# Value products of two tiles side by side, with four probability buffers; maxima over keys by pairs of PSUM banks, with two score banks left

## The reference

```python
B, Lq, H = x_q.shape            # 16, 256, 128
nh = 16; dh = H // nh           # 16 heads of 8
scores = jnp.einsum('bqhd,bkhd->bhqk', q, k) / jnp.sqrt(jnp.float32(dh))
attn = jax.nn.softmax(scores, axis=-1)
out = jnp.einsum('bhqk,bkhd->bqhd', attn, v).reshape(B, Lq, H)
```

## Time and profile before

| what | value |
|---|---|
| median of 3 runs | 6772.17 us (6766.07 to 6781.2) |
| the profiled execution's own time | 6777.38 us |
| its span, first to last instruction | 6775.6 us |
| mean granted TensorE clock | 0.963 of full speed |
| PE busy | 6148.7 us (91%) |
| DVE busy | 4444.0 us (66%) |
| ACT busy | 4234.5 us (62%) |
| POOL busy | 982.1 us (14%) |

### The profile page before, as it was taken

The page is one execution under the profiler, slowest core; times in us unless marked ns, Lnnn a source line. Parts: engine busy times, 40 slices in busy tenths (PEclk is TensorE's granted clock), DMA queues, the critical chain, the costliest instruction groups (busy, mean ns, idle before and its releaser), DMA issues.

```text
span 6775.6 us, 156710 instructions
## 1 busy us (share of the span) xinstructions
PE 6148.7 (91%) x49714; PEld 3142.0 (46%) x49714; DVE 4444.0 (66%) x9848; ACT 4234.5 (62%) x8158; POOL 982.1 (14%) x1660
## 2 busy tenths in 40 slices
PE   6999999999777999999998777799999999979998
PEld 3444444444444444444443344344444444435554
DVE  5777777776555777777775355577777777724333
ACT  3777777777665777777775465566766767642223
POOL 3112112211111111111110011221211211100000
PEclk9999999999998999999999899899999999989998
DMA  2222222221112222222220111222212222101110
GB/s 84 74 71 60 62 76 66 55 73 43 56 56 73 77 66 65 67 73 76 66 64 20 37 56 61 67 56 75 66 52 77 56 63 67 46 32 41 42 42 24
DMA packets 181002, 403.68 MB, mean 60 GB/s; under 512 B 16992, under 2 KB 124560, under 8 KB 166416
## 3 DMA queue, kind: packets, MB, share of 16 engines
q1 hardware_dynamic: 180752, 400.01, 22.0%
HBM read 316.81 MB, written 83.14 MB: 59 GB/s over the span
## 4 chain that ended last, share of the span: by engine, by line
PE 76%; DVE 8%; ACT 6%; issue 6%; DMA 3%; SPq 1%; POOL 1%; DVEq 0%; ACTq 0%; POOLq 0%
PE bank L1112 19%; PE bank L1084 17%; PE bank L1067 16%; DVE MX L1409 3%; DMA QP<-scr_q 3%; PE bank L653 2%; PE bank L1038 2%; PE bank L1033 2%; PE bank L644 2%; PE bank L1099 2%; PE bank L670 1%; PE bank L1088 1%; ACT P L1242 1%; PE bank L582 1%; PE bank L1048 1%
## 5 line engine op out<-in xcount | busy, mean ns | idle before, releaser
L1242 ACT ACTIVATE P<-bank 128x512 f32<-128x512 f32 (+1 forms) x5504 | 3078.5, 596 | 1483.5 <-PE bank L1067 1457.9
L1409 DVE TENSOR_REDUCE MX<-bank 128x1 f32<-128x400 f32 (+1 forms) x6144 | 3214.4, 569 | 1129.9 <-PE bank L1084 1046.9
L1067 PE MATMUL bank<-QP,KP 128*128 128x256 bf16 (+1 forms) x11008 | 2091.0, 277 | 104.2 <-ACT QP L1253 42.9
L1084 PE MATMUL bank<-KP,QP 96*128 96x400 bf16 (+1 forms) x6144 | 2099.1, 342 | 67.6 <-DMA QP<-scr_q 46.7
L1112 PE MATMUL bank<-P,VA 128*25 128x256 f32 (+1 forms) x22016 | 1776.8, 395 | 20.2 <-issue 9.6
L1067 PEld LDWEIGHTS bank<-QP,KP 128*128 128x128 bf16 (+1 forms) x11008 | 1030.2, 101 | 791.0 <-issue 180.0
L1084 PEld LDWEIGHTS bank<-KP,QP 96*128 96x128 bf16 x6144 | 594.2, 97 | 1015.6 <-DVE MX L1409 598.5
L1112 PEld LDWEIGHTS bank<-P,VA 128*25 128x25 f32 (+1 forms) x22016 | 403.8, 102 | 741.7 <-issue 623.8
L1412 DVE TENSOR_REDUCE MX<-bank 128x2 f32<-128x512 f32 x512 | 327.0, 685 | 304.5 <-PE bank L1088 304.4
L1532 POOL COPY VA<-VN 128x416 f32<-128x416 f32 (+1 forms) x320 | 138.9, 434 | 2569.5 <-PE bank L1112 1290.5
L1253 ACT CAST QP<-bank 2x512 bf16<-2x512 f32 x640 | 338.8, 575 | 133.6 <-PE bank L1099 127.6
(11 more groups left out here) (209 smaller groups left out, 4705.5 us busy)
## 6 DMA issues: line engine op xcount, KB each, us to landing
KP<-scr_k SPq DMA_DIRECT2D x192, 900.6 KB
QP<-scr_q SPq DMA_DIRECT2D x960, 48.0 KB
CN<-ctx_n SPq DMA_DIRECT2D x40, 768.0 KB
scr_k<-KSF SPq DMA_DIRECT2D x48, 600.8 KB, 3.3
scr_k<-KSF SPq DMA_DIRECT2D x48, 600.0 KB, 3.4
CT<-ctx_t SPq DMA_DIRECT2D x24, 800.5 KB, 4.4
KP<-scr_ks SPq DMA_DIRECT2D x128, 144.0 KB
scr_q<-QS SPq DMA_DIRECT2D x80, 192.0 KB, 2.1
```

Of the source, the lines that this page charges most:

```text
L1067: last = nc.tensor.matmul(SC[ph.score_bank(2 * (g * ph.nt + t) + half)][0:kt, k * N:(k + 1) * N], KP[g][:, c0:c0 + kt], QP[g][:, h * N:(h ...
L1084: last = nc.tensor.matmul(dst[:, 0:n], QP[g][0:MR, h * N + qt * 128:h * N + qt * 128 + 128], KP[g][0:MR, h * ph.nk + c0:h * ph.nk + c0 + n ...
L1242: nc.scalar.activation(P[v % 2][0:kt, half * 2 * N:(half + 1) * 2 * N], SC[ph.score_bank(2 * (g * ph.nt + t) + half)][0:kt, :], ACT.Exp, s ...
L1409: nc.vector.tensor_reduce(MX[:, r, c:c + 1], src[:, 0:CHUNKS[c][1]], AX.X, ALU.max).then_inc(sem("max_done"), 1)
```

## The change

Three things are changed at once.

- **Value products.** There are four probability buffers (`NP = 4`) in place of two. PE keeps back the value products of a tile and writes those of two tiles one behind the other, in every second tile (where `g * nt + t` is even).
- **Maxima.** Two tensors `MP` of two neighbouring banks each take the place of the three banks `MB`. `maximum` now writes two matmuls of 401 columns, one in each bank of a pair (`SPANS`: the ranges overlap by one key, so that all have 401), and DVE reduces both with one instruction of 2x401 elements. A cross group has 16 of these pairs in place of 32 maxima, a self group 2 (of four matmuls) in place of 4. Pair j waits for the reduction of pair j-2.
- **Scores.** Two score banks are left, one for each half: a score waits for the `Exp` of the same half of the tile before.

`maximum_at` is not edited, but with 16 in place of 32 it now gives the tiles 0 to 10 of a group 2, 1, 2, 1, 2, 1, 2, 1, 2, 1 and 1 pairs, and the third third of a tile, behind the value products, is always empty.

```diff
+NP = 4
+SPANS = [(0, 401), (400, 401), (800, 401), (1200, 401)]
-        self.nm = 2 * G * len(CHUNKS) if self.cross else G
+        self.nm = G * len(SPANS) if self.cross else G // 2
...
-        P = [sb("P%d" % k, [128, G * N], f32) for k in range(2)]
+        P = [sb("P%d" % k, [128, G * N], f32) for k in range(NP)]
...
-        SC, MB, OB, MISC = bank[0:3], bank[3:6], bank[6], bank[7]
+        SC = [ctx.enter_context(nc.psum_tensor("bank%d" % k, [128, 512], f32)) for k in range(2)]
+        MP = [ctx.enter_context(nc.psum_tensor("pair%d" % k, [128, 1024], f32)) for k in range(2)]
...
             def scores(ph, b, g, t, half):
-                u = 2 * (g * ph.nt + t) + half
-                pe.wait_ge(sem("probs_full"), at("probs_full", b, ph.score_before(u) + 1))
+                pe.wait_ge(sem("probs_full"), at("probs_full", b, 2 * (g * ph.nt + t) + half - 1))
...
             def maximum(ph, b, g, j):
-                if j >= len(MB):
-                    pe.wait_ge(sem("max_done"), at("max_done", b, g * ph.nm + j - len(MB) + 1))
-                dst = MB[j % len(MB)]
+                if j >= 2:
+                    pe.wait_ge(sem("max_done"), at("max_done", b, g * ph.nm + j - 1))
+                for k in range(2):
+                    if ph.cross:
+                        h, qt, (c0, n) = j // 4, j // 2 % 2, SPANS[j % 2 * 2 + k]
+                        last = nc.tensor.matmul(MP[j % 2][:, k * 512:k * 512 + n],
...
             def shift_rows(ph, b, g):
-                    dst = MB[1 + half]
+                        c = half * 512 + r * 128
+                        last = nc.tensor.matmul(MP[1][MR:MR + 2, c:c + 128], NMB[g % 2][:, 4 * half + r, :],
...
             def element(el):
-                        if last_tile:
-                            head_values(*last_tile)
-                        last_tile = (ph, b, g, t)
+                        if (g * ph.nt + t) % 2 == 0:
+                            for tile in pending:
+                                head_values(*tile)
+                            pending = []
+                        pending.append((ph, b, g, t))
...
             def exponentials(ph, b, g, t, half):
-                    act.wait_ge(sem("pv_done"), at("pv_done", b, v - 1))
+                    act.wait_ge(sem("pv_done"), at("pv_done", b, v + 1 - NP))
...
             def maximum(ph, b, g, j):
-                    nc.vector.tensor_reduce(MX[:, r, c:c + 1], src[:, 0:CHUNKS[c][1]], AX.X, ALU.max).then_inc(
-                        sem("max_done"), 1)
+                    nc.vector.tensor_reduce(MX[:, r, c:c + 2],
+                                            MP[j % 2][:, :].rearrange("p (t k) -> p t k", t=2)[:, :, 0:SPANS[0][1]],
+                                            AX.X, ALU.max).then_inc(sem("max_done"), 1)
```

More of the change, by code:

```diff
@@ L144, in maximum_at @@
         return [j for j in range(self.nm) if min(j * spread // self.nm, n - 1) == t]
-    def score_bank(self, u):
-        n = 2 * self.nt * NG
-        whole = n - 2 - (n - 2) % 3
-        return u % 3 if u < whole else (u - whole) % 2
-    def score_before(self, u):
-        if u < 3:
-            return (-2, -1, -3)[u]
-        return max(k for k in range(u) if self.score_bank(k) == self.score_bank(u))
     def prep_slots(self, host):
@@ L283, in build @@
     ds = bass.ds
-    start = dict(probs_full=3, pv_done=2, heads_copied=2, mlp_centered=1, mlp_gated=1)
+    start = dict(probs_full=3, pv_done=NP, heads_copied=2, mlp_centered=1, mlp_gated=1)
     start["misc_full"] = 0
@@ L1066, in scores @@
                     c0 = h * ph.nk + t * 128
-                    last = nc.tensor.matmul(SC[ph.score_bank(2 * (g * ph.nt + t) + half)][0:kt, k * N:(k + 1) * N], KP[g][:, c0:c0 + kt],
+                    last = nc.tensor.matmul(SC[half][0:kt, k * N:(k + 1) * N], KP[g][:, c0:c0 + kt],
                                             QP[g][:, h * N:(h + 1) * N], start=True, stop=True)
@@ L1075, in maximum @@
                     pe.wait_ge(sem("packed_loaded%d" % g), at("packed_loaded%d" % g, b, 64))
[L1076 to L1090 removed]
+                elif j == 1:
+                    wait(pe, "rows_done", at("rows_done", b, 2 * g))
+                if j >= 2:
[4 more added lines that the diff above has]
+                        last = nc.tensor.matmul(MP[j % 2][:, k * 512:k * 512 + n],
+                                                QP[g][0:MR, h * N + qt * 128:h * N + qt * 128 + 128],
+                                                KP[g][0:MR, h * ph.nk + c0:h * ph.nk + c0 + n], start=True, stop=True)
+                    else:
+                        h = 2 * j + k
+                        for qt in range(2):
+                            last = nc.tensor.matmul(MP[j % 2][:, (2 * k + qt) * N:(2 * k + qt + 1) * N],
+                                                    QP[g][0:MR, h * N + qt * 128:h * N + qt * 128 + 128],
+                                                    KP[g][0:MR, h * ph.nk:(h + 1) * ph.nk], start=True, stop=True)
                 last.then_inc(sem("max_full"), 1)
@@ L1096, in shift_rows @@
                 for half in range(2):
-                    dst = MB[1 + half]
                     for r in range(4):
-                        last = nc.tensor.matmul(dst[MR:MR + 2, r * 128:(r + 1) * 128], NMB[g % 2][:, 4 * half + r, :],
+                        c = half * 512 + r * 128
+                        last = nc.tensor.matmul(MP[1][MR:MR + 2, c:c + 128], NMB[g % 2][:, 4 * half + r, :],
                                                 IDB[:, :], start=True, stop=True)
@@ L1118, in element @@
                 ph, b = el.ph, el.b
-                last_tile = (el.prev[0], el.prev[1], NG - 1, el.prev[0].nt - 1) if el.prev else None
+                pending = [(el.prev[0], el.prev[1], NG - 1, el.prev[0].nt - k) for k in (2, 1)] if el.prev else []
                 for g in range(NG):
@@ L1240, in exponentials @@
                 if half == 0:
-                    act.wait_ge(sem("pv_done"), at("pv_done", b, v - 1))
-                nc.scalar.activation(P[v % 2][0:kt, half * 2 * N:(half + 1) * 2 * N], SC[ph.score_bank(2 * (g * ph.nt + t) + half)][0:kt, :], ACT.Exp,
+                    act.wait_ge(sem("pv_done"), at("pv_done", b, v + 1 - NP))
+                nc.scalar.activation(P[v % NP][0:kt, half * 2 * N:(half + 1) * 2 * N], SC[half][0:kt, :], ACT.Exp,
                                      scale=SCALE).then_inc(sem("probs_full"), 1)
```

31 lines of the change are left out of this document (11 added, 20 removed).

## The result

The changed kernel takes 6963.59 us (median of 4 runs, 6951.19 to 6985.6) against 6776.68 us for the kernel before in 4 runs beside it (6766.07 to 6782.92): ratio 1.0281, 95% interval 1.0251 to 1.0311. It is slower by some 187 us; 7016 was forecast. The profiled execution took 6951.19 us with a span of 6949.4, so it stands 173.8 us over the span of before.

The account below looks back on a forecast made before the run. PE was taken as the bound. Waits and group ends less pieces gave +5.2 us an element, 250 over 48, less 6 in c2: 6777.4 + 244 = 7021 profiled, 7016 median; range 6920 to 7120, with rivals 6880 to 7170.

Parts of the forecast that it names:

- The bound: Cross stages: PE is the bound, busy 94 to 98%, while ACT and DVE wait for it.
- the two turnarounds: Time until a bank can be used again: 1.16 us for a score bank, 1.60 us for a maxima pair.
- double tiles: Two tiles in cross groups: 3.41 us (even), 3.51 (odd), now 3.24; waits add 1.7 and 2.7 us an element.
- the pair reduction's shorter DVE time: Reducing two banks at once saves DVE some 0.1 us a pair, priced at nothing because PE's time covers it.
- the sum over an element: Cross element: waits 1.7 and 2.7, ends 2.7, less pieces 1.1 and 0.8, together +5.2 us.
- The ends: Ends of cross groups: next group's first scores come 0.77 us later, 0.4 at the last group; 2.7 us an element.
- pieces give back: PE pieces in short tiles fill waits: 1.1 us in group 0, some 0.8 in groups 1 and 3, an element.
- c2's 2.77 us: Wait at the start of a c2 element, taken to swallow the last group's end: 6 us off the sum.
- Rival 1: Whole kernel: waits are covered and the 261 us saved by products together stand, about 6510 us; chance 0.09.
- Rival 2: Whole kernel: pieces fill most waits, so waits and saving cancel, 6750 to 6790 us; chance 0.05.
- Rival 3: a0 and c1: new waits lower the clock too, 147 us more, 7163 us; chance 0.14.
- Rival 4: Group 0: DVE's statistics and norms between reductions delay PE, up to 2 us an element, 7110 us; chance 0.12.

Follow-up runs that it names:

- padded run: 96 small matmuls put ahead of PE's program: in the kernel with pairs and two score banks (6751.90 us), later in the changed kernel (6919.71 us).
- third kernel: Changed kernel with single maxima over the four banks of the pairs, two score banks and products together kept: 6851.42 us, ratio 1.0115 to before.
- fifth kernel: Changed kernel with single maxima over four banks, four in the tile without products and two in the other: 6743.31 us, ratio 0.9948 to before.

## Why the prediction was right, and where it was off

**The bound, and the two turnarounds: right.** 1.16 and 1.60 us are both measured, double tiles are 3.39 and 3.49 for 3.41 and 3.51, and the run with the shorter `Exp` and those with other maxima each moved the one of the two that they should.

**Which edit costs.** Compare stages without stall, each kernel where it has none. Pairs and two score banks together against before: a0 98.4 for 99.3, c1 93.5 for 94.2, c2 97.5 for 98.7. Products together on top of that: 102.3, 97.9, 101.8. So those two save 0.9, 0.7 and 1.2 us an element, 45 us over 48 elements (16 x 2.8), and the products together cost 3.9, 4.4 and 4.3, 202 us (16 x 12.6). In its tiles the change is the sum of the two, 157 us. The prediction priced the pair reduction's shorter DVE time at nothing. It is not nothing in group 0: in c1 it takes 24.94 us with pairs alone (padded run) and 26.18 before.

**The step that was mis-sized** is the sum over an element: +5.2, measured +3.0 (a0), +3.7 (c1), +3.1 (c2), always without stall. Tile by tile in c1 (changed kernel with padding, against before), groups 0 to 3 take 26.11, 23.88, 24.60 and 23.36 us for 26.18, 22.11, 23.76 and 22.14. The ends (tiles 10 to 12) cost 2.4, forecast 2.7: near enough. Tiles 0 to 9 cost 1.3, forecast 2.5 (4.4 of waits less 1.9 that pieces give back). In a0 they cost 1.0 and the ends 2.0. By groups, tiles 0 to 9 of c1 miss the forecast in two places. Group 0, forecast at -0.25 (five waits of 0.17 less 1.1), comes out at -1.1: with pairs alone it is already at -1.56, so the gain that the prediction had at nothing, the pairs', is enough to make up this part. Its tiles 6 and 7 took 4.82 and take 4.08. Group 2, forecast at +0.85, comes out at +0.36, with pairs alone at nothing: there pieces cover waits that I had not counted, and tiles 0 to 3 take 8.04 for 8.11. Groups 1 and 3 together (+2.1 for 1.9) are right. So two terms were mis-sized, the pairs' gain in group 0 and the pieces' cover in group 2. Two smaller slips change nothing: DVE is busy 74% in c2, not 76 to 77%, and 7 us an element on the median of 6772 would give 7108, not 7120.

**The stall: put down wrongly.** I read c2's 2.77 us as a wait that the element has in any case, and took 6 us off the sum for it. It comes with a fetch of instructions and hangs on where the body lies. The change moved it from c2 to c1 (c2 5.5 an element less, c1 3.9 more, c2 again 1.3 more and a0 0.4 by other gaps), which nearly cancels: 16 x (0.4 + 3.9 + 1.3 - 5.5) is 2 us. With the 157 us of the tiles this makes 159 of the 173.8; s1 (+10) and s2 (+5) are about the rest. That the stalls cancel is luck: in the padded run the same tiles are 3.9 us an element better in c1, and the total is 44 us less in spite of the 26.

**Rival 1 (the saving wins)** was refuted, and more sharply than I argued: even with the old banks the saving is zero, since DVE is the next bound. **Rival 2** (they cancel) fails with the waits that pieces leave. **Rival 3 (the clock falls)**: a0 stays at 1.00; c1's 0.98 comes with the stall, and is 1.00 in the padded run with all waits in place. So waits in which PE's loads pause 0.5 us and its matmuls 0.2 to 0.3 did not lower the clock; nor did the 1.38 us that PE stands still for the shift rows in a0 of the padded run. The Trainium skill, "TensorE: Matmul & The Clock Gate", A second HAM failure mode (HAM is the page's name for the clock gate), tells of small idle gaps between groups of matmuls that make the clock swing; with gaps of this size it stayed at 1.00 here. But the rival's mechanism exists in this kernel, and shorter waits than the stall's can set it off: in c2 of the third kernel PE stands still 2.1 us for the shift rows and the clock is at its lower level for 3.4 us behind it, in each of the 14 passes.

```profile
4526.98 1.01 PE L1091 MATMUL pair<-IDB,NMB 128*2 128x128 bf16 x8 [2.12 <-DVE NMB L1419]
```

```profile
4527.10:4530.40 3.30, 3.30 (x28) 1.69 (x26) 1.45 (x9) 2.54 (x6) 0.00 (x0) 0.50 0.02 5
```

**Rival 4 (DVE's pieces on top)** went the other way in group 0, which became shorter in a0 as well (28.35 to 27.56). With single maxima DVE's work does show: that wait for the shift rows (their loads pause 2.39 us) stands in a0 and c2 of the third and fifth kernel.

What stays open: why nine packets a pass stall one stage and leave another alone, and what sets its size (first scores 1.9 to 3.5 us after the matmul before them).

## What to carry to other kernels

A saving on the busiest engine is worth no more than the lead of the next one allows: look in a plain tile at how long each engine needs for that tile's work without a pause, not at its share of the span. When work is bunched, count what then stands in a row on each buffer, and put the free work into the short stretch. Before two kernels with long loop bodies are compared, look at the first instruction of a pass for a stall with no releaser, and compare the stages that have none. A stall on PE is priced with the clock that falls behind it, not by its own length.

## What was not expected of the hardware

- The place of a loop body in PE's program is worth 4 to 5.6 us a pass of some 100 us: 94.2 and 99.1 in c1, 104.2 and 98.7 in c2, for the same tiles. About half of it is the stall, the rest the clock at 1.2 GHz behind it.
- Without the hint at the back edge a pass of a0 costs 10.8 us more (110.1 for 99.3; one execution).
- DVE reduces single banks of 400 elements every 0.50 us in a row, while the mean of one is shown as 568 ns; two banks in one instruction are shown as 989 ns, and three of them in a row take 2.79 us, 0.93 each. The pair saves only 7% of DVE's time.
